# Grouped expert matmul and LoRA layer on one core: another order of the first loads, sums and products

## The reference

```python
# x (128, 64, 1024), ids (128,) of 0..15, weight (16, 1024, 1024), all float32 but ids
y = einsum('bsi,boi->bso', x, weight[ids])            # each sample by its own expert
h = einsum('bsd,nrd->nbsr', y, lora_A)                # lora_A (8, 16, 1024)
lora_out = einsum('nbsr,nor->bso', h, lora_B * (2 * lora_weights)[:, None, None])
out = x + (einsum('bsd,od->bso', y, W) + bias + lora_out)
```

## Time and profile before

| | us |
|---|---|
| median of 3 runs | 1523.1 |
| lowest and highest | 1521.97, 1524.75 |
| the profiled execution | 1520.31 |
| its span, first to last instruction | 1518.6 |

### The profile page before, as it was taken

The page is one execution under the profiler, slowest core; times in us unless marked ns, Lnnn a source line. Parts: engine busy times, 40 slices in busy tenths (PEclk is TensorE's granted clock), DMA queues, the critical chain, the costliest instruction groups (busy, mean ns, idle before and its releaser), DMA issues.

```text
span 1518.6 us, 29617 instructions
## 1 busy us (share of the span) xinstructions
PE 1494.0 (98%) x6354; PEld 1192.3 (79%) x6355; DVE 783.4 (52%) x1192; ACT 393.5 (26%) x493; POOL 460.9 (30%) x645
## 2 busy tenths in 40 slices
PE   6989999999999999999999999999999999999998
PEld 3768888888888888888888888888888888888887
DVE  6687666477787277388853333333333433333332
ACT  4244333344444234244431111111111101111010
POOL 4355334433434523525102112112122121221211
PEclk9999999999999999999999999999999999999999
DMA  8988667566787566569835555555455554555554
GB/s 203 327 242 233 162 179 207 164 185 185 201 226 199 167 183 163 178 193 233 211 115 156 144 139 141 136 140 145 132 139 147 140 145 132 141 145 136 141 142 97
DMA packets 172737, 257.90 MB, mean 170 GB/s; under 512 B 31648, under 2 KB 135584, under 8 KB 172704
## 3 DMA queue, kind: packets, MB, share of 16 engines
q1 hardware_dynamic: 130000, 139.14, 35.9%
q10 hardware_dynamic: 22384, 72.76, 16.3%
q0 software_dynamic: 20320, 45.65, 10.4%
HBM read 181.93 MB, written 75.50 MB: 170 GB/s over the span
## 4 chain that ended last, share of the span: by engine, by line
PE 93%; DMA 3%; DVE 2%; SPq 1%; issue 1%; ACT 0%; DVEq 0%; POOL 0%; ACTq 0%; POOLq 0%
PE ps L753 31%; PE ps L755 31%; PE ps L754 31%; DMA x_raw<-in_x_dram 1%; DMA b_raw<-in_L_ffn_lora_B_dram 1%; SPq L207 1%; DMA weff<-fold_sb 1%; DVE w_lo L596 1%; DMA base_sb<-in_L_ffn_W_dram 1%; DVE w_turn L539 0%; SPq L196 0%; SPq L214 0%; DVE fold_sb L655 0%; DVE x_lo L634 0%; DVE x_turn L627 0%
## 5 line engine op out<-in xcount | busy, mean ns | idle before, releaser
L753 PE MATMUL ps<-w_hi,x_hi 128*128 (+1 forms) x2096 | 828.9, 395 | 6.6 <-issue 3.7
L754 PE MATMUL ps<-w_lo,x_hi 128*128 (+1 forms) x2096 | 828.2, 395 | 0.0
L755 PE MATMUL ps<-w_hi,x_lo 128*128 (+1 forms) x2096 | 828.2, 395 | 0.0
L753 PEld LDWEIGHTS ps<-w_hi,x_hi 128*128 128x128 f32 x2096 | 393.5, 188 | 105.8 <-issue 4.8
L755 PEld LDWEIGHTS ps<-w_hi,x_lo 128*128 128x128 f32 x2096 | 393.5, 188 | 96.7
L754 PEld LDWEIGHTS ps<-w_lo,x_hi 128*128 128x128 f32 x2096 | 393.6, 188 | 96.3
L627 DVE STREAM_TRANSPOSE x_turn<-x_raw 128x256 f32<-128x256 f32 x544 | 193.7, 414 | 510.5 <-DMA x_raw<-y_scr 456.0
L207 POOL DMA_DIRECT2D x_raw<-in_x_dram x552 | 294.7, 534 | 399.9 <-DVE x_turn L627 262.2
L421 ACT ACTIVATE x_hi<-x_turn 128x512 fp32r<-128x512 f32 x272 | 167.2, 630 | 697.4 <-DVE x_turn L627 681.0
L396 POOL TENSOR_TENSOR stage<-stage,w_place 128x1024 f32<-128x1024 f32 x64 | 152.8, 2388 | 611.1 <-DMA stage<-in_x_dram 611.1
L634 DVE TENSOR_TENSOR x_lo<-x_turn,x_hi 128x512 fp32r<-128x512 f32 x272 | 180.5, 691 | 133.1 <-ACT x_hi L421 128.4
(11 more groups left out here) (69 smaller groups left out, 38.3 us busy)
## 6 DMA issues: line engine op xcount, KB each, us to landing
w_place<-in_L_cond_weight_dram SPq DMA_DIRECT2D x480, 128.0 KB, 4.2
y_scr<-stage ACTq DMA_DIRECT2D x72, 512.0 KB, 4.1
x_raw<-in_x_dram POOLq DMA_DIRECT2D x552, 64.0 KB, 3.6
x_raw<-y_scr SPq DMA_DIRECT2D x512, 64.0 KB, 2.4
stage<-in_x_dram SPq DMA_DIRECT2D x128, 256.0 KB, 3.7
out_dram<-stage ACTq DMA_DIRECT2D x126, 256.0 KB, 3.0
base_sb<-in_L_ffn_W_dram POOLq DMA_DIRECT2D x8, 512.0 KB, 11.2
weff<-fold_sb POOLq DMA_DIRECT2D x8, 512.0 KB, 11.2
```

Source lines behind the costliest of these rows:

```text
L753: mm(ps[b][:, cols], x_hi[b][:, t, :], hi, start=t == 0, stop=False)
L754: mm(ps[b][:, cols], x_hi[b][:, t, :], lo, start=False, stop=False)
L755: last = mm(ps[b][:, cols], x_lo[b][:, t, :], hi, start=False, stop=t == KT - 1)
```

## The change

It touches the beginning, and the order of the three products in every tile.

- **First loads.** B is loaded whole, as the first transfer of ACT's queue; A whole, on SP's. The first three loads of W0 (c0, c1, c2) are all issued before the tables, quarters 2 and 3 on ACT's queue behind B. Only c3 comes after the tables.
- **Tables.** DVE's second turn of W0 (chunk 1) comes behind the tables; the first stays ahead of them.
- **Bases.** Eight buffers instead of six: `stage0` and `stage1` are the fifth and sixth. POOL issues bases 0 to 5, then 6 and 7, then x of tile 3, and no base waits for a sum. x of tile 4 is loaded by POOL behind the stores instead of by SP, and x of tiles 6 and 7 wait until six chunks of W1 are turned.
- **Sums.** DVE makes sums 0 to 5 ahead of x of tile 2, sums 6 and 7 behind it. ACT waits for all eight sums before it moves y of slot 0 to `stage0`.
- **Second expert.** Behind x of the fourth tile (tile 3) DVE and ACT begin with W1; its chunks 0 to 3 come ahead of x of tile 4, chunks 4 to 7 behind it.
- **PE.** Five folds ahead of slot 0, three between its halves. In each half the eight x_hi·w_hi matmuls come first, then eight x_lo·w_hi, then eight x_hi·w_lo, and each group waits for its own operand; the wait for x in front of a slot is gone.

The core of the diff:

```diff
-    BASES = 6
+    BASES = 8
...
+        base_sb = base_sb[:4] + stage + base_sb[4:]
...
             sp.dma_start(ids_i[:, :], ids.rearrange("(s a) -> s a", a=1)).then_inc(ids_loaded, 16)
-            load_first(sp, 0, (0, 1), w0_loaded)
-            load_b(sp, 0)
-            load_a(sp, 0)
-            load_first(sp, 1, (0, 1), w0_loaded)
+            for c in range(2):
+                load_first(sp, c, (0, 1), w0_loaded)
+            sp.dma_start(a_sb[:, :], lora_a.rearrange("n r d -> (n r) d")).then_inc(a_loaded, 16)
+            load_first(sp, 2, (0, 1), w0_loaded)
             sp.wait_ge(tables, 1)
...
-            for c in range(2, LOADS):
-                load_first(sp, c, (0, 1), w0_loaded)
+            load_first(sp, 3, (0, 1), w0_loaded)
...
-            for h in range(2):
-                load_sample(sp, RING, 0, h, first_loaded[0])
...
             def load_base(f):
-                if f >= BASES:
-                    pool.wait_ge(base_added, f - BASES + 1)
...
             pool.wait_ge(b_turned, 1)
-            for f in range(4):
+            for f in range(6):
+                load_base(f)
+            pool.wait_ge(w_turned, 6)
+            for f in range(6, FOLDS):
                 load_base(f)
             for h in range(2):
                 load_sample(pool, 3, 3, h, first_rest[3])
-            pool.wait_ge(w_turned, 6)
-            for f in range(4, FOLDS):
-                load_base(f)
             for f in range(FOLDS):
                 pool.wait_ge(base_added, f + 1)
                 pool.dma_start(fold_rows(weff, f), fold_sb[:, f, :]).then_inc(weff_ready, 16)
+            for h in range(2):
+                load_sample(pool, RING, 0, h, first_rest[0])
             load_x(RING + 1, 1)
+
+            pool.wait_ge(w_turned, 2 * CHUNKS - 2)
             load_x(RING + 2, 2)
...
-            load_first(act, 0, (2, 3), w0_loaded)
-            load_b(act, 1)
-            load_a(act, 1)
-            load_first(act, 1, (2, 3), w0_loaded)
+            act.dma_start(b_raw[:, :, :, :].rearrange("p n f r -> p n (f r)"),
+                          lora_b.rearrange("n (p f) r -> p n (f r)", f=FOLDS)).then_inc(b_loaded, 16)
+            for c in range(LOADS - 1):
+                load_first(act, c, (2, 3), w0_loaded)
...
+            act.wait_ge(base_added, FOLDS)
             move_y(0, 0, 0)
             round_x(3, 3)
+
+            act.wait_ge(weff_ready, 16 * FOLDS)
+            round_w(1, 1, range(0, CHUNKS // 2))
             round_x(4, 0)
-
-            act.wait_ge(weff_ready, 16 * FOLDS)
-            round_w(1, 1)
+            round_w(1, 1, range(CHUNKS // 2, CHUNKS))
...
+            for f in range(6):
+                add_base(f)
             prepare_first(2)
-            for f in range(FOLDS):
...
+            for f in range(6, FOLDS):
+                add_base(f)
             prepare_first(3)
+            prepare_w(1, 1, range(0, CHUNKS // 2))
             prepare_first(4)
-            prepare_w(1, 1)
+            prepare_w(1, 1, range(CHUNKS // 2, CHUNKS))
...
+                    pe.wait_ge(w_rounded, ready + (half + 1) * CHUNKS // 2)
+                    for t in range(KT):
+                        if half == 0 and t % (KT // 2) == 0:
+                            pe.wait_ge(x_rounded, n * 2 + (1 + t // (KT // 2)))
+                        mm(ps[b][:, cols], x_hi[b][:, t, :], hi[t], start=t == 0, stop=False)
+                    if half == 0:
+                        pe.wait_ge(x_ready, n * 2 + 2)
+                    for t in range(KT):
+                        mm(ps[b][:, cols], x_lo[b][:, t, :], hi[t], start=False, stop=False)
                     pe.wait_ge(w_ready, ready + (half + 1) * CHUNKS // 2)
...
                     for t in range(KT):
-                        hi = w_hi[:, bass.ds(par, 1), t, cols].rearrange("p a m -> p (a m)")
-                        lo = w_lo[:, bass.ds(par, 1), t, cols].rearrange("p a m -> p (a m)")
-                        mm(ps[b][:, cols], x_hi[b][:, t, :], hi, start=t == 0, stop=False)
-                        mm(ps[b][:, cols], x_hi[b][:, t, :], lo, start=False, stop=False)
-                        last = mm(ps[b][:, cols], x_lo[b][:, t, :], hi, start=False, stop=t == KT - 1)
+                        last = mm(ps[b][:, cols], x_hi[b][:, t, :], lo[t], start=False, stop=t == KT - 1)
```

75 lines of the change are left out of this document (33 added, 42 removed).

## The result

| | before | after |
|---|---|---|
| median of the runs made side by side, us | 1521.97 (6 runs) | 1510.6 (6 runs) |
| lowest and highest | 1520.28, 1524.75 | 1508.02, 1513.52 |
| the profiled execution | 1520.31 | 1511.33 |

The ratio is 0.9923, with a 95% interval of 0.9909 to 0.9937: faster. The two profiled executions differ by 8.98 us, just the 8.9 of the sum. This agreement is a coincidence: two steps of the sum were wrong and cancelled, and the experiments put most of the gain in another part of the change than the sum had it.

What follows compares the result with a forecast made beforehand. TensorE, busy 98% of the span, bounds the kernel. Slot 6 at 92.3 instead of 99.18 gives 6.9 us, kept clock 2.0, together 8.9; from the median of 1523.1 this makes 1514.2, range 1511.0 to 1520.5.

Steps and rivals of the forecast that it cites:

- First loads: Kernel's start: B and c0 share the DMA engines by packets from 3 us; B lands at 9.6 to 11.6, c0 15.5.
- Tables: Routing tables behind W0's first turn: ready at 16.9 against 16.73 before, so the earlier B gains them nothing.
- the 8.9 of the sum: Total gain forecast in us: 6.9 from slot 6 starting earlier plus 2.0 from its kept clock.
- Tile 0: First tile on TensorE: starts at 28.0 after about 4 us idle, low clock costs 1.6, second half follows at once.
- Rival (b): Beginning: c0 early, VectorE 2 to 3 us sooner, no low clock in the first tile; 1510.5 us, chance 0.06.
- Bases and sums: Before W1: eight buffers remove a 15.53 us wait; last store issued at 54.7, W1's first rounding 64.3 instead of 73.35.
- Tile 4 inside W1: VectorE's path to slot 6: tile 4 adds 2.8 us; x ready at 90.4, 2.2 ahead of TensorE at 92.6.
- Low clock at slot 6: TensorE's pause before slot 6 shrinks to about 1 us, so full clock is kept, saving 2.0 us.
- Order of the products: Every tile on TensorE: four more waits, same 48 matmuls, costed at nothing, spacing staying 0.233 us.
- rival (c): Matmul stream of all tiles: the added waits stand exposed, 24 us, so 1538 us; chance 0.09.
- rival (d): After slot 6: the pause only moves to slot 8, since x8 waits behind held x6 and x7; 1523, chance 0.04.
- Rival (a): Stores before W1 land late, the last at 70; low clock stays, gain 3.1, 1520.0 us; chance 0.13.

Runs made afterwards that it cites:

- b_on_sp: The changed kernel with B whole on SP's queue, directly behind ids, instead of first on ScalarE's queue; 1510.7 us.
- act_store: The changed kernel with the eight stores of weff issued on ScalarE's queue instead of GpSimd's; 1514.4 us.
- x4_a: The changed kernel with x of tile 4 ahead of all of W1, and A between c0 and c1 on SP's queue; 1507.2 us.
- x4_first: The changed kernel with x of tile 4, loaded by SP, moved back ahead of all of W1; 1508.1 us.

## Why the prediction was right and wrong

- **First loads: wrong, and the first step to fail.** The term was the overlap of B with c0: both queues share "from 3 us", which gave B at 9.6 to 11.6 and c0 at 15.5. B was sorted from 6.78 and c0 turned at 11.16. From 3 to 4 us ScalarE's queue passed 583 packets and SP's none, and b_on_sp brings B back to about 9.2 by its place alone. The rate was off too: from 3 to 11 us 271 GB/s were moved, not 240. Equal packets held between pieces of one size (328 to 304) and later (act_store), but not for B's small pieces once both queues ran (727 to 321 in b_on_sp). The prediction had 11.8 as the other end for c0, from sharing by bytes: about the right number, but the head start and the rate made it.
- **Tables: wrong as a consequence.** "The earlier B buys the tables nothing" and the tables at 16.9: they stood at 12.33. The prediction had the first split at 19.3, 1.0 later than before; it came at 14.25. At x of tile 1 VectorE was 4.1 us earlier than before (36.27 against 40.39), and the forecast of 39.1 was missed by 2.8. Rival (b) said this, with 2 to 3 us and 1510.5, and had a chance of 0.06.
- **Tile 0: right in its mechanism**, wrong in size. The first product depends on x_hi, the second half follows at once. The forecast 28.0 with 4 us of pause and low clock was 25.50 with none, since the folds waited for A, whose wait the sum lacked, and ended just then. That wait (4.33 us) and the slow folds behind it (10.51 us where 20 took 8.82 in x4_a) are about as long as the 4 us and 1.6 us that the sum had ahead of and in tile 0: luck again.
- **Bases and sums: the step that had the wrong owner.** The eighth sum ends at 51.5 (forecast 54.4), the last store took 10.47 (9.6), the first rounding came at 62.28 (64.3). But the 15.53 us of the earlier trace rows were read as the cause, and undoing the middle cost 1.6 us (not clear of the noise), not most of 8.9. The wait was itself fed by the late tables, through x of tile 2 and the first sum.
- **Tile 4 inside W1: costed rightly, read wrongly.** The 2.8 us were in the sum, called free because TensorE would come later. It came at 87.4 and not at 92.6, so they stood on the path; x4_first gets 2.7 back.
- **Low clock at slot 6: wrong.** I took 2.0 us off for a pause of 1 us. The pause was 2.64, and 24 matmuls took 7.25 us (90.00 to 97.25) where 0.233 each gives 5.6: 1.7 lost. Slot 6 was 2.3 us earlier than forecast. The two nearly cancel, which is why the profiled pair fits 8.9.
- **Order of the products, rival (c), rival (d): right.** The spacing is unchanged. VectorE waited for x of tiles 7 and 8 (5.60 and 4.97 us), and TensorE saw none of it. Rival (a) did not come.
- **From the sum to the median: a miss of its own.** The profiled execution of before is one of its fastest (1520.31; the medians in four later sets, 53 runs, are 1521.5 to 1521.9), and the 1523.1 of three runs was high. With 1521.97 the same sum would give 1513.1. The remaining 2.5 us are the difference between one pair of executions (8.98) and the medians (11.0 to 11.4). Granted clocks over the span are 0.995 to 0.998 in runs of before and mostly 0.998 to 1.000 after, so some of it may be low clock in stretches that the one profile of before doesn't show; this was not settled.

## What to carry to other kernels

Look for the stretch in which the DMA engines idle while work that needs them is still unissued, and ask what its issue waits for: here the routing tables, through B, so that the long wait for a base buffer later on was mostly a symptom. Before you let two transfers share from a kernel's start, look when each queue passes its first packets: here c0, behind ids, began nearly 2 us after B, and B had the engines almost to itself. When a chain waits for a store, put the independent work into that wait. A further queue for the stores did not help here: it took its packets from theirs.
